# First attention of a two-block layer: exponentials over three heads in place of two, and one accumulator bank in place of two

## The reference, cut to what matters

```python
q = q / jnp.maximum(jnp.linalg.norm(q, axis=-1, keepdims=True), EPS_NORM)
k = k / jnp.maximum(jnp.linalg.norm(k, axis=-1, keepdims=True), EPS_NORM)
attn = jnp.einsum('bhqd,bhkd->bhqk', q, k) * HEAD_DIM ** 0.5
attn = jax.nn.softmax(attn, axis=-1)
out = jnp.einsum('bhqk,bhkd->bhqd', attn, v)
...
x = x + attention(xn) + fp4_ffn(xn)      # first block
x = x + attention1(xn) + experts(xn)     # second block: 4 heads, then 160 experts
```

## Time and profile before

| | |
|---|---|
| runs | 921.47, 915.98, 920.35 us; median 920.35 us |
| the profiled execution | 917.9 us, of it 915.7 us from the first to the last instruction (the span) |
| granted PE clock in it | 0.983 of full speed on average |
| busy | PE 834.2 us, ACT 717.8 us, DVE 667.3 us, POOL 34.7 us |

### The profile page before, as it was taken

How to read it: one execution, slowest core, us unless ns; L and a number is a source line. 1 busy time by engine, 2 the same in 40 slices (tenths; PEclk the granted TensorE clock), 3 DMA queues, 4 the chain that set the end, 5 groups by cost and what they waited for, 6 DMA issues and landing times.

```text
span 915.7 us, 15851 instructions
## 1 busy us (share of the span) xinstructions
PE 834.2 (91%) x4516; PEld 524.2 (57%) x4516; DVE 667.3 (73%) x1358; ACT 717.8 (78%) x1263; POOL 34.7 (4%) x41
## 2 busy tenths in 40 slices
PE   4779989897999989897999999999999999999997
PEld 2421212171121229674777777777777777777775
DVE  5754734145683016973999999999999999999997
ACT  2779999857999985564888788877887778888886
POOL 1700000000000000400000000000000000000000
PEclk9969999998999999998999999999999999999999
DMA  4000000000000000006777777777877777777883
GB/s 117 1 1 1 1 1 1 1 1 0 1 1 1 1 1 2 12 30 175 188 199 197 192 200 195 195 198 191 204 194 192 194 193 195 195 199 194 199 201 96
DMA packets 66776, 99.88 MB, mean 109 GB/s; under 512 B 29270, under 2 KB 45942, under 8 KB 66742
## 3 DMA queue, kind: packets, MB, share of 16 engines
q1 hardware_dynamic: 66742, 99.44, 42.4%
HBM read 97.04 MB, written 2.36 MB: 109 GB/s over the span
## 4 chain that ended last, share of the span: by engine, by line
PE 48%; ACT 18%; DMA 11%; DVE 8%; issue 8%; SPq 5%; DVEq 1%; ACTq 0%
ACT E L418 15%; DMA wg_raw<-in_L_ffn_w_gate_dram 11%; PE PS L1335 6%; PE PS L1337 5%; PE PS L1336 5%; PE PS L1342 5%; PE PS L1344 5%; PE PS L1343 5%; PE PS L1045 4%; SPq L223 4%; PE PS L1030 2%; PE PS L1122 2%; DVE HM L936 2%; ACT SI L562 2%; PE PS L1314 1%
## 5 line engine op out<-in xcount | busy, mean ns | idle before, releaser
L562 ACT ACTIVATE SI<-PS 128x512 f32<-128x512 f32 x320 | 191.6, 599 | 86.9 <-PE PS L1337 86.7
L936 DVE TENSOR_TENSOR HM<-SI,CWB 128x512 f32<-128x512 f32 x320 | 221.5, 692 | 39.2 <-ACT SI L562 16.6
L418 ACT ACTIVATE E<-PS 128x1024 f32<-128x1024 f32 x256 | 241.6, 1024 | 8.7 <-PE PS L1030 7.4
L941 DVE TENSOR_TENSOR HLo<-HM,HH 128x512 fp32r<-128x512 f32 x320 | 219.1, 685 | 0.2
L358 ACT ACTIVATE HH<-HM 128x512 fp32r<-128x512 f32 x320 | 199.4, 623 | 3.7 <-DVE HM L936 3.7
L1045 PE MATMUL PS<-E,VS 128*32 128x512 f32 x1024 | 139.2, 616 | 0.4 <-ACT E L418 0.4
L1335 PE MATMUL PS<-XH,wgH 128*128 128x512 f32 x320 | 134.5, 420 | 0.0
L1342 PE MATMUL PS<-HH,wdH 128*128 128x512 f32 x320 | 128.4, 401 | 1.0 <-DVE HLo L941 1.0
L1344 PE MATMUL PS<-HH,wdL 128*128 128x512 f32 x320 | 127.1, 397 | 0.0
L1336 PE MATMUL PS<-XL,wgH 128*128 128x512 f32 x320 | 127.0, 397 | 0.0
L1337 PE MATMUL PS<-XH,wgL 128*128 128x512 f32 x320 | 126.8, 396 | 0.0
(11 more groups left out here) (214 smaller groups left out, 832.3 us busy)
## 6 DMA issues: line engine op xcount, KB each, us to landing
CWB<-combine_weights SPq DMA_DIRECT2D x320, 256.0 KB, 3.9
wg_raw<-in_L_ffn_w_gate_dram SPq DMA_DIRECT2D x80, 64.0 KB, 3.4
wd_raw<-in_L_ffn_w_down_dram SPq DMA_DIRECT2D x80, 64.0 KB, 3.7
X<-in_L_attn_x_dram SPq DMA_DIRECT2D x4, 256.0 KB, 3.8
combine_weights<-CWT SPq DMA_DIRECT2D x2, 512.0 KB, 2.9
out_dram<-X SPq DMA_DIRECT2D x4, 256.0 KB, 2.9
combine_weights<-CWT SPq DMA_DIRECT2D x2, 128.0 KB, 3.8
qkvw_raw<-in_L_attn_qkv_w_dram SPq DMA_DIRECT2D x1, 192.0 KB, 3.8
```

The costliest lines, as they stand in the source:

```text
L418: nc.scalar.activation(E[:, (2 * st + u) % NE_SLOTS, :], PS[:, 2 * u:2 * u + 2, :], ACT.Exp, scale=SCALE0).then_inc(S["exp_act"], 1)
L562: nc.scalar.activation(SI[:, slot % 2, :], bank(4 + slot % 2), ACT.Silu).then_inc(S["s_act"], 1)
L936: TT(HM[:, slot % 4, :], SI[:, slot % 2, :], CWB[:, q, half, CH * c:CH * c + CH], ALU.mult)\
L941: TT(HLo[:, slot % 4, :], HM[:, slot % 4, :], HH[:, slot % 4, :].bitcast(F32), ALU.subtract)\
```

## The change

The banks are dealt out anew. Banks 0 to 2 and 3 to 5 are two sets for the scores; bank 6 is the only accumulator of the value product, and bank 7 the only bank for its transposes.

The unit of the scores and the exponentials is no longer half a step. The 256 single-head scores of a batch (64 steps of four heads) are numbered through and cut into 86 pieces of three (`TRIOS`, the last with one): `scores(b, g)` makes three heads into one set of banks, and one exponential of 1536 columns takes them, into one of the six slots of `E` (`RING`). A trio crosses the border of a step three times in four. `after(st)` says behind which trio the value product of a step is issued: two trios behind the one that holds its last head, and three for the first step of a group. `values` no longer waits for exponentials itself; the wait in the `scores` before it covers that. With one accumulator the first `values` of a group waits for DVE's copy of the group before it, not of the one before that, and `out_T(m)` waits for `divide(m - 1)`, not for `divide(m - 2)`. `out_T` is issued behind the third step of the next group.

```diff
-        NE_SLOTS = 8
-        E = sb("E", [P, NE_SLOTS, 1024], F32, ph0)
+        E = sb("E", [P, RING, 3, CH], F32, ph0)
...
+        UNITS = STEPS0 * HG
+        TRIOS = -(-UNITS // 3)
...
             def exponentials(b):
-                for st in range(STEPS0 * b, STEPS0 * b + STEPS0):
-                    for u in range(2):
-                        if st >= NE_SLOTS // 2:
-                            act.wait_ge(S["av_pe"], st - NE_SLOTS // 2 + 1)
-                        act.wait_ge(S["qk_pe"], 2 * st + u + 1)
-                        nc.scalar.activation(E[:, (2 * st + u) % NE_SLOTS, :], PS[:, 2 * u:2 * u + 2, :], ACT.Exp,
-                                             scale=SCALE0).then_inc(S["exp_act"], 1)
+                for g in range(TRIOS):
+                    n, w = TRIOS * b + g, min(3, UNITS - 3 * g)
+                    if g >= RING:
+                        act.wait_ge(S["av_pe"], STEPS0 * b + (3 * (g - RING) + 2) // HG + 1)
+                    act.wait_ge(S["qk_pe"], n + 1)
+                    nc.scalar.activation(E[:, n % RING, 0:w, :], PS[:, 3 * (n % 2):3 * (n % 2) + w, :], ACT.Exp,
+                                         scale=SCALE0).then_inc(S["exp_act"], 1)
...
-                src = bank(6 + m % 2).rearrange("p (t c w) -> p (t c) w", t=GT, c=HG)
+                src = bank(7).rearrange("p (t c w) -> p (t c) w", t=GT, c=HG)
...
-                nc.vector.tensor_copy(OS[:, m % 2, :], bank(4 + m % 2)).then_inc(S["oc_dve"], 1)
+                nc.vector.tensor_copy(OS[:, m % 2, :], bank(6)).then_inc(S["oc_dve"], 1)
...
-            def scores(st, u):
+            def scores(b, g):
...
-                if st >= 1:
-                    pe.wait_ge(S["exp_act"], 2 * st + u - 1)
-                for h in range(2 * u, 2 * u + 2):
+                n = TRIOS * b + g
+                if n >= 2:
+                    pe.wait_ge(S["exp_act"], n - 1)
+                for u in range(3 * g, min(3 * g + 3, UNITS)):
+                    st, h = u // HG, u % HG
+                    p, c, k = st // (CB * NB), st // NB % CB, st % NB
                     r = slice(32 * h, 32 * h + 32)
-                    last = MM(bank(h), KT[r, n, P * k:P * k + P], QT[r, n, CH * c:CH * c + CH],
+                    last = MM(bank(3 * (n % 2) + u % 3), KT[r, p, P * k:P * k + P], QT[r, p, CH * c:CH * c + CH],
                               start=True, stop=True)
...
-                if k == 0 and m >= 2:
-                    pe.wait_ge(S["oc_dve"], m - 1)
+                if k == 0 and m >= 1:
+                    pe.wait_ge(S["oc_dve"], m)
...
             def out_T(m):
                 pe.wait_ge(S["oc_dve"], m + 1)
-                if m >= 2:
-                    pe.wait_ge(S["ao_dve"], m - 1)
+                if m >= 1:
+                    pe.wait_ge(S["ao_dve"], m)
...
-            LAG = 2
+            def after(st):
+                return (HG * st + HG - 1) // 3 + (3 if st % NB == 0 and st else 2)
 
             def attention(b):
...
+                done = 0
+                for g in range(TRIOS):
+                    scores(b, g)
+                    while after(done) <= g:
+                        values(b, done)
+                        done += 1
+                        if done % NB == 3 and done > NB:
+                            out_T(GRP * b + done // NB - 1)
+                pe.wait_ge(S["exp_act"], TRIOS * (b + 1))
+                for st in range(done, STEPS0):
+                    values(b, st)
+                out_T(GRP * b + GRP - 1)
```

More of the change, by code:

```diff
@@ L30, in two_block_layer_kernel @@
     CB = N // CH
+    RING = 6
     H0, HD0 = 16, 8
@@ L1021, in heads_T, with values @@
                 last.then_inc(S["qkT_pe"], 1)
-            def scores(st, u):
-                n, c, k = st // (CB * NB) % NHG, st // NB % CB, st % NB
-                if st >= 1:
-                    pe.wait_ge(S["exp_act"], 2 * st + u - 1)
-                for h in range(2 * u, 2 * u + 2):
+            def scores(b, g):
[5 more added lines that the diff above has]
+                    p, c, k = st // (CB * NB), st // NB % CB, st % NB
                     r = slice(32 * h, 32 * h + 32)
-                    last = MM(bank(h), KT[r, n, P * k:P * k + P], QT[r, n, CH * c:CH * c + CH],
+                    last = MM(bank(3 * (n % 2) + u % 3), KT[r, p, P * k:P * k + P], QT[r, p, CH * c:CH * c + CH],
                               start=True, stop=True)
                 last.then_inc(S["qk_pe"], 1)
-            def values(st):
-                m, k = st // NB, st % NB
+            def values(b, st):
+                m, k = GRP * b + st // NB, st % NB
                 s = m // CB % 2
-                pe.wait_ge(S["exp_act"], 2 * st + 2)
                 if st % (CB * NB) == 0:
                     pe.wait_ge(S["vs_pool"], m // CB + 1)
-                if k == 0 and m >= 2:
-                    pe.wait_ge(S["oc_dve"], m - 1)
+                if k == 0 and m >= 1:
+                    pe.wait_ge(S["oc_dve"], m)
                 for c in range(HG):
-                    e = E[:, (2 * st + c // 2) % NE_SLOTS, CH * (c % 2):CH * (c % 2) + CH]
-                    last = MM(PS[32 * c:32 * c + 32, 4 + m % 2, :], VS[:, s, k, c, :], e,
+                    u = HG * st + c
+                    e = E[:, (TRIOS * b + u // 3) % RING, u % 3, :]
+                    last = MM(PS[32 * c:32 * c + 32, 6, :], VS[:, s, k, c, :], e,
                               start=(k == 0), stop=(k == NB - 1), skip_group_check=True)
@@ L1050, in out_T @@
                 pe.wait_ge(S["oc_dve"], m + 1)
-                if m >= 2:
-                    pe.wait_ge(S["ao_dve"], m - 1)
+                if m >= 1:
+                    pe.wait_ge(S["ao_dve"], m)
                 for j in range(GT):
-                    last = TR(bank(6 + m % 2)[:, P * j:P * j + P], OS[:, m % 2, P * j:P * j + P], ident[:, :])
+                    last = TR(bank(7)[:, P * j:P * j + P], OS[:, m % 2, P * j:P * j + P], ident[:, :])
                 last.then_inc(S["oT_pe"], 1)
-            LAG = 2
+            def after(st):
+                return (HG * st + HG - 1) // 3 + (3 if st % NB == 0 and st else 2)
             def attention(b):
-                st0, st1 = STEPS0 * b, STEPS0 * b + STEPS0
-                for st in range(st0, st1):
-                    scores(st, 0)
-                    if st >= st0 + LAG:
-                        values(st - LAG)
-                    scores(st, 1)
-                    if st % NB == LAG + 2 and st > st0 + NB:
-                        out_T(st // NB - 1)
-                for st in range(st1 - LAG, st1):
-                    values(st)
-                out_T(st1 // NB - 1)
+                done = 0
[10 more added lines that the diff above has]
+                out_T(GRP * b + GRP - 1)
             h_T(0)
@@ L1094, in _ @@
             attention(0)
-            pe.wait_ge(S["exp_act"], 2 * STEPS0)
             pe.wait_ge(S["ao_dve"], GRP)
```

## The result

The changed kernel takes **911.25 us** (median of 6 runs, 910.47 to 913.06); beside it the kernel before took 920.23 us. The ratio is 0.9932, 95% interval 0.9909 to 0.9956. A second set of six runs gave 909.26 against 916.38 us, ratio 0.9923 (0.9896 to 0.9949). So it is faster by 0.7 to 0.8%, which lies within the 1% that I called no change, and the forecast of 911.1 us is hit. The saving itself is less sure than that: 9.0 us between these medians, 7.1 us in the second set, 4.8 us between the two profiled executions, where 9.3 us was forecast. And the time was hit with the wrong terms, as the traces show.

What follows compares the result with a forecast made beforehand. ACT's exponentials were taken to bound both attention batches. Batches -10.4 us and ends +1.1 us gave -9.3 us, from 917.9 to 908.6 us for the profiled execution, 911.1 us as a median; range 905 to 918 us.

Steps and rivals of the forecast that it cites:

- The exponentials: Both attention batches: 1536 columns take 1.449 us, every 1.368; a batch without gaps 116.88 us, 7.82 us less for both.
- PE in the steady state: PE late 0.14 us at groups 2, 3, 5, 6 and 0.54 us at 3, 6: 1.64 us gaps per batch.
- The start: First exponentials of each batch, with PE at half clock: gaps of 2.0 us in batch 0, 0.9 in batch 1.
- One accumulator: A group's first value step waits for DVE's copy of the group before; hidden, costed at nothing.
- The margin at group 2: Copy of group 2, behind the quantised weights: about 1.3 us late, still hidden by 1.0 us.
- The end: Behind each batch: last transposes wait for `divide(6)` and start about 0.53 us later; 1.1 us more for both.
- rival 3: PE's clock: rise at the start later, 913 us, chance 0.12; lasting stretch at 1.2 GHz, tens of us, chance 0.01.
- Rival 1: Fixed cost of an exponential not saved, a trio every 1.449 us: 919 us, slower by 1.3 us; chance 0.07.
- rival 2: DVE's copy holds PE at group borders for 0.7 us plus release: costs 4 us, 915 us; chance 0.12.
- rival 4: PE's bunching costs nothing and the starts are no worse than before: 907 us; chance 0.18.

Runs made afterwards that it cites:

- experiment 2: The changed kernel with each trio's exponential split into two ACTIVATEs, over two banks and over one: 922.38 us.
- experiment 3: The kernel before (exponentials of two heads) with only the accumulator and the transposes cut to one bank each: 921.77 us beside 917.1.
- experiment 7: The changed kernel with every value step issued two trios behind, also at the borders in place of three: 904.06 us.
- experiment 8: The changed kernel with two trios of delay throughout and each batch's last transposes in a score bank: 899.2 us (ratio 0.9807) and 902.12 us (0.9803).
- experiment 6: The changed kernel with the transposes of each batch's last group in a free score bank, not waiting for `divide(6)`: 905.37 us.
- experiment 5: The changed kernel with filler matmuls that nothing reads on PE at each batch's end, before and behind the last transposes: 913.85 us.
- experiment 4: The changed kernel with batch 1's first exponential also waiting for batch 0's value steps, as before the change: 916.04 us.
- experiment 1: The changed kernel again, without an edit, beside the kernel before: 909.26 us, ratio 0.9923.
- experiment 9: The kernel of experiment 8 with the quantising of the down weights moved behind group 2's copy on DVE: 898.4 us, ratio 0.9779.
- experiment 10: The kernel of experiment 9 with filler matmuls that nothing reads at the batches' starts: 898.28 us, ratio 0.9775.
- experiment 11: The kernel before with the value products of seven in eight steps on only 128 of 512 queries, so not this layer's time: 939.84 us.

## Why the prediction held, point by point

The total was right to 0.2 us, and so was its mechanism as a whole (exponentials, less lateness, one hidden copy, a wait at the end). Several terms were not, and that the total came out so close is luck: two errors of 6 us cancelled.

- **"The exponentials": mis-sized, twice.** The record was right (1.45 us when nothing is in front of it, 1.449 predicted). The spacing of 1024 columns was not: I took the mean over 16 exponentials, 0.943 us, as the unstalled one, but one in four of them came 0.14 to 0.17 us late for PE, which a grouped row of the timeline swallows as if it were ACT's own time. Unstalled it is 0.903, the trio's 1.330 and not 1.368 (3.1 us less a batch), and the fixed cost 0.05 and not 0.09 us (experiment 2). By the Trainium skill (ScalarE: Activation LUTs, What ACT_TABLE_LOAD costs) the spacing would be 1.373 us, as an estimate; the measured 1.330 and 0.903 fit its column rate, with an overlap of some 0.12 us of the 1.45 us record where it has 0.093. So a batch without lateness is 113.8 us and was predicted as 116.88. It also means that the gain isn't where I put it: of batch 0's 8.0 us, 1.9 come from fewer instructions, 6.1 from PE being late less.
- **"PE in the steady state": the places right, the sizes small.** Predicted 0.14 us at exponentials 26 and 37 and 0.54 at 38, and 32 trios on. Measured over the spacing of 1.330: 0.38, 0.28 and 0.58, then 0.66, 0.28 and 0.58 us in batch 0, 2.8 us for a predicted 1.64. The shorter spacing explains a part: the slack of two trios shrinks by 0.08 us. In batch 1 exponential 37 came 1.93 us late, of which 1.7 are clock.
- **"The start"**: 0.7 us in batch 0 (2.0 predicted), since the clock rose 6.1 us after the first exponential, and 2.0 us in batch 1 (0.9 predicted), where it fell late and stayed down until 212.97, 8.9 us after the first.
- **"One accumulator": right, and costed rightly at nothing** in the changed kernel (and alone, experiment 3: no new wait at a border). In its trace no value step waits for DVE. The margin at group 2 was as thin as said: with one trio of delay less that border has the longest wait, 0.8 us, and the only one that makes an exponential late by more than 0.3 us (experiments 7 and 8). The Trainium skill (Perfetto Trace Analysis, Optimizing Tensor Performance, Matmuls) asks for rotating banks between independent groups; here the copy is hidden in one bank at all 14 borders, as the delay covers it. With the shorter delay PE does wait, at 11 of them, as the rule has it, but ACT, which bounds the batch, feels it at one. What I missed is the price of the protection: the third trio of delay leaves PE idle twice in a row at four borders of a batch.
- **"The end": right.** +0.53 us each predicted, +0.54 and +0.59 measured; experiments 3 and 6 confirm the cause. Here too the idle time had a follower that I didn't name: the clock falls behind it.
- **The clock, rival 3: priced wrongly.** I held against it a stretch at clock 1.00 with PE busy 4.79 of 7.00 us. That stretch ends at 212.00, with PE idle since 211.11 and before that for 1.31 us, and the clock fell 0.13 us later; the stretch behind it (0.50, shown above with the result) was in the trace that I had, and spoke for the rival. In the changed kernel it fell at one border and behind both ends: 1.7 + 1.5 + 2.9 = 6.1 us. Experiments 5 and 6 take the falls at the ends away in two different ways, and with them 1.5 and 2.9 us of clock.
- **The table load**: no term, -1.3 us (experiment 4).

Rebuilt with the measured terms (us): against the forecast, spacing -6.2, starts -0.2, later gaps +1.1 in batch 0 and, without the clock, +0.8 in batch 1, small latenesses +0.4, ends +0.1, clock +6.1, table -1.3; together +0.8, and -9.3 + 0.8 = -8.5, as the stretches give. An error of 6.2 us in the spacing and one of 6.1 in the clock cancelled. Rival 1 (919 us from a spacing of 1.449) is refuted by the single spacings, and rival 2 (the copy at the borders) by the trace, in which no value step waits for DVE, and by experiment 3; rival 4 is refuted by the waits at 26 to 38.

**What stays open.** Which borders lose the clock. Behind the starts, the batches of the changed kernel and of experiments 1, 2 and 4 to 10 have 20 falls, and each lies in the second of two idle times of PE of 0.8 to 1.0 us or within 1.1 us behind it, with at most one value step between the two. There are 51 such pairs in these traces, so 31 had no fall, and no fall came at any of the 149 single idle times of 0.7 to 1.0 us. The kernel before and experiment 3 have no idle time of that length and no fall. So such a pair is needed here, and it isn't enough. Batch 0 has the same code in the changed kernel and in experiments 1, 4, 5 and 6, and it fell at no border in the changed kernel, 1 and 6 (117.5, 117.5, 117.6 us), but at three of them in 4 and 5 (122.6 and 122.6). In those two the first exponential stood at 55.2 and 54.6 us, in the others at 53.3 to 53.9, and PE's first stretch at half clock began later (45.2 and 44.7 us against 42.3 to 43.1). Something of when things happen may decide, and no experiment varied that alone. That the pair matters is supported by experiments 7 to 10: with two trios of delay the pairs are gone but for the one at group 2's copy, and with the copy moved that one too, and the falls went with them.

## What to carry to other kernels

Take the unstalled spacing of an engine's instructions from the single starts of a chain whose producers were ready, never from the mean of a grouped row: lateness of 0.15 us in one of four instructions hid there, and lateness of all sizes was most of what the change gained. The commonest difference isn't safe either: it was 0.920 us before, since no chain lasted long. A kernel that is bound by one engine still pays for how the others idle: here the gain of 0.7% became 2.2% (898.4 us) by spreading PE's value steps evenly, giving the last transposes a bank of their own, and moving a copy ahead of long DVE work. When a margin has to be bought with a later start of work, ask what stands idle in the meantime and whether the work then comes in a bunch.

## What the runs showed of the hardware

- Less work for PE made the kernel slower: 0.55 and 0.51 of the clock and 10 to 12 us a batch (experiment 11, one execution). With matmuls that nothing reads it stayed at 1.00 behind both batches (experiment 5) and at a batch's start (experiment 10).
- Inside a batch the clock fell only at two idle times of PE of 0.8 to 1.0 us close together, at 20 of 51 such pairs, and at none of 149 single ones. A fall slows what comes next: 3.45 us for two value steps that take 1.92.
- Exponentials back to back start every 0.903 us (1024 columns), 1.330 us (1536) and 0.477 us (the 512 columns behind 1024), though their records are 1.02, 1.45 to 1.66 and 0.75 us long. In a chain they start 0.1 us or more before the end of the one before, so a record's length is no measure of its cost. Behind a break the next spacing is 0.017 us longer (0.920 and 1.346 us).
- The load of ACT's table can go ahead of the exponential's wait or behind it, by the number of that exponential's waits: 1.3 us at a change of function.
